# Perceiver block with a selective scan: GpSimd computes u times B for the next state, into two state buffers

## The reference

```
xc    = silu(causal 4-tap conv(x @ x_proj_w.T))      # 1024 channels
B, C  = x @ B_proj_w.T, x @ C_proj_w.T               # 16 states each
delta = softplus(x @ dt_proj_w.T + dt_proj_b)
h_t   = exp(delta_t * A) * h_(t-1) + delta_t * B_t * xc_t   # per channel and state
y_t   = sum over the states of h_t * C_t, + D * xc_t
x     = x + y @ out_proj_w.T
```

## Time and profile before

| | us |
|---|---|
| median of 3 runs | 1515.77 |
| lowest and highest run | 1514.64, 1516.62 |
| span of the profiled execution, first to last instruction | 1514.9 |
| DVE busy in that span | 1157.1 |
| PE busy | 1281.5 |
| ACT busy | 599.0 |
| POOL busy | 0.2 |

### The profile page before, as it was taken

How to read it: one execution, slowest core, us unless ns; L and a number is a source line. 1 busy time by engine, 2 the same in 40 slices (tenths; PEclk the granted TensorE clock), 3 DMA queues, 4 the chain that set the end, 5 groups by cost and what they waited for, 6 DMA issues and landing times.

```text
span 1514.9 us, 16115 instructions
## 1 busy us (share of the span) xinstructions
PE 1281.5 (85%) x6400; PEld 965.9 (64%) x6400; DVE 1157.1 (76%) x1001; ACT 599.0 (40%) x1229; POOL 0.2 (0%) x4
## 2 busy tenths in 40 slices
PE   6998578868859758858758898999999999998998
PEld 4776446646536547536537586777777777676775
DVE  1201899998999998999998848979888888446554
ACT  4432754554655535745536611131313131022220
POOL 0000000000000000000000000000000000000000
PEclk9999878988978978979879789999999999999999
DMA  7333013324013324013314201222222312114553
GB/s 247 101 121 127 6 25 116 104 63 133 8 49 91 118 54 128 10 49 110 89 57 145 91 22 35 86 61 70 56 77 63 84 49 63 56 44 152 168 160 103
DMA packets 95930, 128.47 MB, mean 85 GB/s; under 512 B 4976, under 2 KB 70640, under 8 KB 95856
## 3 DMA queue, kind: packets, MB, share of 16 engines
q1 hardware_dynamic: 95856, 127.45, 27.9%
HBM read 125.21 MB, written 2.23 MB: 84 GB/s over the span
## 4 chain that ended last, share of the span: by engine, by line
DVE 55%; PE 31%; ACT 8%; issue 3%; DMA 2%; DVEq 0%; ACTq 0%; SPq 0%
DVE state L1077 16%; PE bank L634 11%; DVE y_acc L1084 8%; DVE state L1074 8%; DVE state L1080 7%; PE bank L591 6%; PE bank L665 6%; ACT decay L855 4%; DVE x_tokens L1179 3%; DVE w_lo L1161 2%; DMA queries_ctx<-in_dt_t 2%; PE bank L520 2%; PE bank L545 2%; DVE hidden L1168 2%; DVE hidden L1167 2%
## 5 line engine op out<-in xcount | busy, mean ns | idle before, releaser
L1077 DVE TENSOR_TENSOR_SCAN state<-decay,state 128x2048 f32<-128x2048 f32 x64 | 282.9, 4420 | 8.3 <-ACT decay L855 7.2
L665 PE MATMUL bank<-w_down,hidden 128*128 128x512 f32 x512 | 232.1, 596 | 5.2 <-DVE x_tokens L1179 5.2
L634 PE MATMUL bank<-x_hi,w_hi 128*128 128x256 f32 x1024 | 192.6, 312 | 12.2 <-DVE hidden L1168 7.5
L855 ACT ACTIVATE decay<-delta_odd,params 128x256 f32<-128x256 f32 x256 | 106.3, 498 | 197.7 <-DVE state L1077 186.8
L634 PEld LDWEIGHTS bank<-x_hi,w_hi 128*128 128x128 f32 x1024 | 150.3, 198 | 43.5 <-issue 30.4
L520 PE MATMUL bank<-ctx,queries_ctx 128*128 128x256 f32 x512 | 151.8, 449 | 22.2 <-ACT queries_ctx L748 22.2
L634 PE MATMUL bank<-x_hi,w_lo 128*128 128x256 f32 x1024 | 168.9, 288 | 0.0
L634 PE MATMUL bank<-x_lo,w_hi 128*128 128x256 f32 x1024 | 168.7, 288 | 0.0
L902 ACT ACTIVATE hidden<-bank 128x512 f32<-128x512 f32 x64 | 38.0, 594 | 327.6 <-PE bank L665 321.5
L665 PEld LDWEIGHTS bank<-w_down,hidden 128*128 128x128 f32 x512 | 93.3, 191 | 100.5 <-issue 94.2
L1084 DVE TENSOR_TENSOR y_acc<-y_acc,state 128x2048 f32<-128x2048 f32 x64 | 146.7, 2292 | 2.3
(11 more groups left out here) (128 smaller groups left out, 1328.1 us busy)
## 6 DMA issues: line engine op xcount, KB each, us to landing
ctx<-in_ctx_t SPq DMA_DIRECT2D x32, 512.0 KB, 6.3
ctx<-in_ctx_n SPq DMA_DIRECT2D x32, 512.0 KB, 3.5
bc_bcast<-bc_scratch SPq DMA_DIRECT2D x64, 256.0 KB, 5.1
raw_w<-in_eg_t SPq DMA_DIRECT2D x32, 512.0 KB, 4.3
raw_w<-in_eu_t SPq DMA_DIRECT2D x32, 512.0 KB, 4.0
w_down<-in_ed_t SPq DMA_DIRECT2D x32, 512.0 KB, 4.8
queries_ctx<-in_dt_t SPq DMA_DIRECT2D x4, 2048.0 KB, 10.0
queries_ctx<-in_xp_t SPq DMA_DIRECT2D x4, 2048.0 KB, 14.8
```

What stands on the lines that cost most here:

```text
L634: mm = pe.matmul(o, w[a](k), x[b](k), start=(q == 0), stop=(q == len(terms) - 1))
L665: mm = pe.matmul(b[t][:, :], hid[j % 2][:, i * GT + t * P:i * GT + (t + 1) * P], w_dn[k % 2][:, i, :], start=(i == 0), stop=(i == IC - 1))
L855: ins = act.activation(dA[n % 2][:, k * GT:(k + 1) * GT], dlt[g % 2][:, k, :], ACT.Exp, scale=par[:, c:c + 1])
L1077: dve.tensor_tensor_scan(h, dA[n % 2], h, 0.0, ALU.mult, ALU.add).then_inc(scan_rd, 1)
```

## The change

POOL gets a program that, for every one of the 64 steps, multiplies u by B into one of two state tiles. DVE's part 0 of `scan_step` falls away, and its scan waits for POOL's result. POOL waits for the start of a group (`dl_rdy`), for B and C of the step (`bc_in`), and for the end of step n-2, whose tile it overwrites (`step_done`).

The second state tile of 8 KB per partition is paid for with other tiles: `conv_in` loses its own place and lies on the first columns of the attention's `probs`, so its zero columns are written anew in each group (`conv_pads`), and ACT waits for that; the combine weights and the routing tiles are allocated at the end, above the region that the early stage used.

```
-        hs_ = sb("state", SW)
+        hs_ = [sb(f"state_{s}", SW) for s in range(2)]
...
-            xi_ = sb("conv_in", 2 * 2 * XP, stack=early)
-            xi = [xi_[:, s * 2 * XP:(s + 1) * 2 * XP].rearrange("p (k t) -> p k t", t=T + TAPS - 1) for s in range(2)]
+            xi = [pp_[:, s * 2 * XP:(s + 1) * 2 * XP].rearrange("p (k t) -> p k t", t=T + TAPS - 1) for s in range(2)]
...
             def proj_x(g, k0):
...
-                act.wait_ge(pad_rdy, 1)
+                act.wait_ge(pad_rdy, g + 1)
...
+        @block.gpsimd
+        def _(pool):
+            for n in range(G * NS):
+                g = n // NS
+                if n % NS == 0:
+                    pool.wait_ge(dl_rdy, g + 1)
+                pool.wait_ge(bc_in[n % 2], 16 * (n // 2 + 1))
+                if n >= 2:
+                    pool.wait_ge(step_done, n - 1)
+                bs = bcs[n % 2][:, 0, :].unsqueeze(1).to_broadcast([P, NBK, GT])
+                pool.tensor_tensor(hs_[n % 2][:, :].rearrange("p (k t) -> p k t", k=NBK), u[g % 2], bs, ALU.mult)\
+                    .then_inc(ub_rdy, 1)
...
+            def conv_pads():
+                for s in range(2):
+                    ins = dve.memset(xi[s][:, :, 0:TAPS - 1], 0.0)
+                ins.then_inc(pad_rdy, 1)
...
             def scan_step(g, j, parts=range(SCAN_PARTS)):
                 n = g * NS + j
-                h = hs_[:, :]
+                h = hs_[n % 2][:, :]
                 h3 = h.rearrange("p (k t) -> p k t", k=NBK)
-                bs, cs = (bcs[n % 2][:, w, :].unsqueeze(1).to_broadcast([P, NBK, GT]) for w in range(2))
-                if 0 in parts:
-                    dve.wait_ge(bc_in[n % 2], 16 * (n // 2 + 1))
-                    step(dve.tensor_tensor(h3, u[g % 2], bs, ALU.mult))
+                cs = bcs[n % 2][:, 1, :].unsqueeze(1).to_broadcast([P, NBK, GT])
                 if 1 in parts:
+                    dve.wait_ge(ub_rdy, n + 1)
                     dve.wait_ge(da_rdy, n + 1)
...
-            for s in range(2):
-                ins = dve.memset(xi[s][:, :, 0:TAPS - 1], 0.0)
-            ins.then_inc(pad_rdy, 1)
...
             add_tiles(0)
+            conv_pads()
             dve.nop().then_inc(x1_rdy, 1)
...
                 add_tiles(g + 1)
+                conv_pads()
                 dve.nop().then_inc(x1_rdy, 1)
```

More of the change, by code:

```diff
@@ L145, in perceiver_block @@
         bcT = nrm_[0:2 * NS, 0:GT]
-        comb_ = sb("comb", G * NT * E)
         xT_ = sb("normed_t", DC * GT)
@@ L163, in perceiver_block @@
         ident = par[:, C_ID:C_ID + P]
-        lgs = [sb(f"route_logits_{c}", NT * E)[:, :] for c in range(G)]
-        sc, sfc, gs = (sb(f"route_{n}", NT * E)[:, :] for n in ("score", "choice", "group"))
         st_ = sb("stats", 6 * G * NT)
@@ L231, in perceiver_block @@
         rank_ = sb("rank_scratch", 2 * NT * E * E)
+        comb_ = sb("comb", G * NT * E)
+        lgs = [sb(f"route_logits_{c}", NT * E)[:, :] for c in range(G)]
+        sc, sfc, gs = (sb(f"route_{n}", NT * E)[:, :] for n in ("score", "choice", "group"))
         rk1, rk2 = (rank_[:, k * NT * E * E:(k + 1) * NT * E * E] for k in range(2))
@@ L291, in perceiver_block @@
         scan_rd = sem("decay_read")
+        ub_rdy = sem("state_input_ready")
         step_done = sem("scan_step_done")
```

## The result

The changed kernel takes 1604.55 us (median of 4, 1598.17 to 1605.11) against 1515.82 us before: 1.0576 times the time, interval 1.0555 to 1.0597. The forecast was 1602.

What follows compares the result with a forecast made beforehand. DVE bounds the first three groups' scans beside attention, PE the last group beside the experts. 3 x 27.3 + 4 x 1.0 = +85.9 us on the 1514.9 us span, plus 0.9, gives 1602 us; range 1565 to 1644, widened 1480 to 1660.

Steps and rivals of the forecast that it cites:

- What bounds: DVE sets the time in the first three groups' scans beside attention, PE in the fourth beside the experts.
- Step (1): POOL's multiply n waits for step n-2 and B's DMA (5.1 us to land); DVE's step falls to 9.11 us.
- Step (2): POOL's multiply of u by B takes 4.42 us, between 2.29 and 7.5 us.
- Step (3): In scan steps, POOL's SBUF-reading multiply and DVE's two-SBUF-tensor instructions exclude each other; 4.42 us added to every step.
- Rival (a): Free overlap of POOL and DVE: scan spacing under 10 us, 1427 us in all; chance 0.17.
- rival (b): Sharing by the element: scan and both multiplies stretched, 10.7 us per state, 1488 us up to no change; chance 0.11.
- rival (c): POOL much dearer: 7.5 us per multiply with exclusion, 1723 us in all; chance 0.02.
- Step (4): Sum under exclusion: 13.53 us per step, 27.3 us per group in the first three, 1.0 us per state 0; +85.9 us.
- The cover I named for state 14: Beside the projections, one late multiply hides under additions and norms of 342 to 348 us reading at most one SBUF tensor.
- Projections: States 14 and 15 beside the projections: two multiplies cost 4.42 us against 4.64 before; nothing added.
- The last group: 15 states beside the experts: a 4.42 us block costs DVE about 2 us, what it saves; nothing, between -10 and +30.
- the 10 us that I had named as a sign of being wrong: A change over 10 us from first to last expert job would show the claim of no expert-stretch cost wrong.

Runs made afterwards that it cites:

- the loads: On the changed kernel's layout, VectorE doing all multiplies, POOL fills an unused tile each step: two-tensor multiply 1694.37 us, copy 1557.70 us, memset 1515.91 us.
- the load with two reads: Changed kernel's layout, all multiplies on VectorE; POOL multiplies two halves of the out_proj weights into an unused tile each step, nobody waiting: 1694.37 us.
- the load that copies: Changed kernel's layout, all multiplies on VectorE; POOL copies one 128x2048 fp32 tensor into an unused tile each step, nobody waiting: 1557.70 us.

## Why the prediction was right, point by point

**What bounds.** Right: the first three stretches carry all of the loss that can be put down to POOL.

**Step (1), what POOL waits for.** Right in the trace: 683 us of its idle time end with B's DMA. That this doesn't matter under exclusion held within 21 us only: an earlier B moves POOL beside instructions that read PSUM, and exclusion doesn't hold for those.

**Step (2), the price of POOL's multiply.** Forecast 4.42 us; where nothing holds it, it takes 4.50 (the shortest of 64), and what DVE loses is 4.20. That it came so close is partly luck: the ratio of the tiny memsets, 1.7, would have given 3.9 us where the ratio is 4.50 / 2.29 = 1.96, and 4.42 was the row of another operation. Why DVE loses 0.3 us less than POOL's own time isn't shown. The Trainium skill's 4497 ns (GPSIMD Engine Reference, Performance versus the Vector engine) agrees.

**Step (3), exclusion.** Right, and shown by the loads: two reads and one read hold DVE, writing alone does not, and the same DVE work is untouched when POOL is idle. The rows of before had left it open, and the prediction said so. The Trainium skill, SBUF — State Buffer, Who interferes with whom, says this for a DVE instruction with two SBUF inputs against a GpSimd instruction that reads, and excepts one that only writes; the traces agree with both halves. Rival (a) falls with 13.3 us a step, rival (b) with whole blocks of 4.2 us beside scans of 4.42 us that are not stretched at all, rival (c) with 4.50 us.

**Step (4), the sum.** Per group +28.3 was forecast and +30.0, +30.1, +29.6 measured. Two errors went against each other. The block is 4.20, not 4.42: -2.9 us for 13 states. And state 14's multiply did not go under the norm: POOL started it beside the last step, at 363.53, where B had landed, so it held one more addition to y:

```profile
365.20 6.47 DVE L1101 TENSOR_TENSOR y_acc<-y_acc,state 128x2048 f32<-128x2048 f32 x1
371.70 1.29 DVE L1045 TENSOR_TENSOR x_tokens<-x_tokens,bank 128x512 f32<-128x512 f32 x2
```

So there are 14 blocks for 13 multiplies saved behind state 0, and 1.25 us for state 0 (its scan starts 4.77 us after the memset instead of 3.52): 14 x 4.20 - 13 x 2.32 + 1.25 = 29.9. At a group's start POOL runs two multiplies in a row, and the second holds the first scan for 4.25 us; that is the block that state 1 would have met. That the total came out within 3 us is partly luck: the three stretches are 5 us above their forecast, and the rest of the span is 3 us below its own, by differences that runs without POOL's multiplies show too.

The cover I named for state 14 was also wrong in kind. I took the norm's instructions as free because they read one SBUF tensor. Two of them, which take 0.54 us alone, were held beside a POOL multiply: one at 885.6 us, ahead of the last group's scan, took 4.25 us, and one in the last group 4.85:

```profile
L1015 DVE TENSOR_SCALAR normed<-x_tokens,mean_var,rstd x16: 535/545/4851, 124.3 to 1422.5; 128x512 f32<-128x512 f32 x16
```

This fits what the prediction had read from the earlier trace rows, a single tensor read both ways, though no run tests it apart. It doesn't go for every instruction with one SBUF input: the norm's statistics keep 673 to 697 ns in all 24 of the load with two reads, eight of them beside a POOL multiply. No instruction fed from PSUM was seen held: in that load and with B a step earlier `neg_max` keeps 691 to 692 ns in all 32, 24 of them beside a POOL multiply (in the changed kernel none is), and in the changed kernel line 1184 keeps 675 to 689 ns in all 64, six of them beside one.

**Projections.** Forecast nothing, measured +2.3 us in the first group. PE's granted clock differs at their start. Windows of after, the stretch ahead of the first matmul of line 591 and the first piece of it (columns as in the earlier trace rows):

```profile
371.70:384.00 12.30, 5.59 (x16) 2.81 (x16) 11.32 (x15) 1.86 (x4) 5.72 (x1) 0.50 0.74 261
384.00:389.40 5.40, 5.39 (x17) 4.54 (x18) 5.37 (x2) 0.00 (x0) 2.57 (x1) 0.69 0.60 237
```

The same of before:

```profile
342.20:353.80 11.60, 5.63 (x17) 2.85 (x17) 10.88 (x13) 1.86 (x4) 0.00 (x0) 0.50 0.76 254
353.80:357.60 3.80, 3.80 (x18) 3.36 (x19) 3.73 (x3) 0.02 (x1) 0.00 (x0) 0.98 0.96 382
```

In both the clock is 0.50 (1.2 GHz) ahead of the projections. Before, it is back at 2.4 GHz when they start; after, it rises some us into them, and their first piece takes 5.4 us instead of 3.8: 1.6 of the 2.3 us. But POOL is not the cause. The run with two tiles and POOL idle has the same slow start, and its first projections take 54.2 us; the load that copies has the fast one, and takes 51.9. The first piece of line 591 with two tiles and POOL idle:

```profile
352.57:357.90 5.33, 5.33 (x15) 4.39 (x16) 5.26 (x3) 0.00 (x0) 0.00 (x0) 0.60 0.74 292
```

and in the load that copies:

```profile
367.20:371.10 3.90, 3.90 (x18) 3.46 (x19) 3.83 (x3) 0.20 (x1) 0.00 (x0) 1.00 0.97 385
```

Nor is it the idle time of PE ahead of the norm's transposes, 10.8 us before and 17.2 after: it is 10.4 us with two tiles and POOL idle, where the start is slow, and 12.4 in the load that copies, where it is fast. What decides when the clock rises in an execution stays open; the +2.3 us are no effect of the change that the runs show.

**The last group.** Forecast nothing, between -10 and +30. The stretch came out 3.8 us shorter than before and 1.3 us longer than with two tiles and POOL idle (664.1 against 662.8): nothing, as forecast. From the first to the last expert job it is 634.9 us against 644.3 before, just inside the 10 us that I had named as a sign of being wrong, and 639.3 with POOL idle. A block there costs less than the 2 us I took from DVE's occupancy: with POOL in the last group alone it is 0.97 us on the scan, and that run gains 7.6 us, where I had expected no more than 6. Part of a block falls into time in which DVE would wait for ACT; how much was not separated.

## What to carry to other kernels

Before work goes from a full VectorE to an idle GpSimd, list what VectorE still runs meanwhile: if that reads two SBUF tensors (here all three instructions of a step), GpSimd's time is added, not hidden, and at 4.2 us of block for 2.3 us saved the move loses. It can pay where VectorE has idle time or reads PSUM: beside the experts it gained 0.45%. Four short GpSimd instructions lost less than one long one beside the attention (1566 against 1605 us), since part of them went beside PSUM-fed instructions and into short idle times. In a trace, look at the durations of the neighbour's instructions (maximum against minimum of one line), since the waiting stands inside them and not in the idle time. And before a difference of a few us in one stretch is put down to a change, look at the same stretch in a run that lacks the cause: here it took 2.3 us of the projections off POOL's account.

## What the runs showed of the hardware that was not expected

- Both engines book their waiting as duration: one 128x2048 multiply on POOL reads 4.50 to 8.48 us, one scan on DVE 4.41 to 8.77.
- With several short POOL instructions queued, the two engines alternate one by one; POOL never got two in while a DVE instruction was ready in the unit shown.
- POOL copies 128x2048 fp32 in 1.89 us and sets it in 1.81 us, so reading a second tensor adds 2.6 us to its multiply.
- A DVE instruction with one SBUF input can be held too: of the norm's `TENSOR_SCALAR` of 128x512 (0.54 us) one took 4.85 us beside POOL's multiply, while the statistics of the same tile keep 0.69 us.
